# Sinkhorn scaling in a mixing layer: two vectors and two fixed copies of the matrix in place of a matrix scaled in place

## What is computed

```
x_norm = x * rsqrt(mean(x * x) + eps)
H_res_logits = (x_norm @ W_res.T).reshape(B, T, 4, 4) + H_res_base
...
Z = H_res_logits / 0.1
for _ in range(50):                      # Sinkhorn, in logs
    u = -logsumexp(Z + v[..., None, :], axis=-1)
    v = -logsumexp(Z + u[..., :, None], axis=-2)
H_res = exp(Z + u[..., :, None] + v[..., None, :])
H_res = (1 - g) * I + g * H_res          # g = sigmoid(gate)
x_mixed = einsum('btij,btjc->btic', H_res, x_streams)
out = x_mixed + einsum('btc,btn->btnc', (x_pre @ W_branch), H_post)
```

## Time and profile before

| | |
|---|---|
| median of three runs | 2952.16 us (2950.13 to 2953.05) |
| the profiled execution, its own time | 2949.29 us |
| its span, first to last instruction | 2947.6 us |
| mean granted TensorE clock | 0.941 |
| busy share PE, DVE, ACT, POOL | 88%, 62%, 37%, 38% |
| loop of 49 rounds on DVE | 1207.42 to 1384.23 us of the span |
| the mixing of the 16 tiles | 1385.27 to 1491.4 us |

### The profile page before, as it was taken

How to read it: one execution, slowest core, us unless ns; L and a number is a source line. 1 busy time by engine, 2 the same in 40 slices (tenths; PEclk the granted TensorE clock), 3 DMA queues, 4 the chain that set the end, 5 groups by cost and what they waited for, 6 DMA issues and landing times. The chain is left out here.

```text
span 2947.6 us, 50657 instructions
## 1 busy us (share of the span) xinstructions
PE 2588.3 (88%) x15056; PEld 1807.8 (61%) x15056; DVE 1821.9 (62%) x4485; ACT 1082.8 (37%) x2317; POOL 1123.7 (38%) x801
## 2 busy tenths in 40 slices
PE   7999997999998899553759999978999987996999
PEld 6665644765553688542647555536665644885887
DVE  5677775567774433788766766764677773215443
ACT  2345554154555211442511545542355554002000
POOL 7456553555664000000044655536456552002110
PEclk9999998999999899666979999989999998998999
DMA  4323312432320521000134322223232313434111
GB/s 163 102 84 84 95 49 68 147 92 66 102 69 30 180 71 43 0 0 7 80 128 135 86 83 85 79 73 110 77 96 78 103 42 138 141 121 150 65 64 44
DMA packets 121079, 252.95 MB, mean 86 GB/s; under 512 B 12720, under 2 KB 39728, under 8 KB 120880
## 3 DMA queue, kind: packets, MB, share of 16 engines
q1 hardware_dynamic: 120912, 251.03, 26.7%
HBM read 166.57 MB, written 84.41 MB: 85 GB/s over the span
## 5 line engine op out<-in xcount | busy, mean ns | idle before, releaser
L617 ACT ACTIVATE a_prob<-a_pst 128x512 f32<-128x512 f32 (+3 forms) x1536 | 660.9, 493 | 572.2 <-PE a_pst L898 566.4
L710 DVE CUSTOM_DVE_ANT_0 a_psh<-a_psh,a_edge 128x128 f32<-128x128 f32 (+3 forms) x1024 | 480.1, 516 | 198.0 <-PE a_psh L851 170.6
L851 PE MATMUL a_psh<-a_kst,a_qst 127*128 127x512 f32 (+3 forms) x1536 | 485.3, 364 | 26.3 <-DVE a_mx L710 14.4
L898 PE MATMUL a_pst<-a_qst,a_kst 128*128 128x512 f32 (+2 forms) x1536 | 487.2, 372 | 23.1 <-DMA a_qst<-rowmax 18.6
L517 POOL TENSOR_TENSOR a_prob<-a_prob 128x2048 f32<-128x2048 f32 (+1 forms) x96 | 405.6, 4225 | 242.5 <-PE a_ppv L914 242.5
L851 PEld LDWEIGHTS a_psh<-a_kst,a_qst 127*128 127x128 f32 x1536 | 272.4, 189 | 240.2 <-DVE a_mx L713 92.7
L713 DVE TENSOR_REDUCE a_mx<-a_psh 128x1 f32<-128x512 f32 x512 | 329.3, 685 | 127.3 <-PE a_psh L851 126.2
L898 PEld LDWEIGHTS a_pst<-a_qst,a_kst 128*128 128x128 f32 x1536 | 287.5, 194 | 163.9 <-ACT a_prob L617 103.5
L914 PE MATMUL a_ppv<-a_prob,a_vg 128*32 128x512 f32 (+3 forms) x3072 | 319.2, 502 | 0.0
L502 POOL TENSOR_SCALAR_AFFINE_SELECT a_prob<-a_prob 128x512 f32<-128x512 f32 x256 | 161.9, 639 | 188.1 <-ACT a_prob L617 187.9
L927 PE MATMUL a_pden<-a_prob,a_ones 128*32 128x512 f32 (+3 forms) x2304 | 220.1, 475 | 14.1 <-POOL a_prob L517 14.1
(11 more groups left out here) (227 smaller groups left out, 4164.1 us busy)
## 6 DMA issues: line engine op xcount, KB each, us to landing
a_qst<-q SPq DMA_DIRECT2D x192, 256.0 KB, 4.5
a_wraw<-in_wqkv SPq DMA_DIRECT2D x52, 512.0 KB, 4.3
q<-a_stg_hi SPq DMA_DIRECT2D x64, 256.0 KB, 2.1
q<-a_stg_lo SPq DMA_DIRECT2D x64, 256.0 KB, 2.4
a_kst<-kT SPq DMA_DIRECT2D x96, 128.0 KB, 2.6
oT<-a_oT SPq DMA_DIRECT2D x32, 256.0 KB, 2.4
oT<-a_vT SPq DMA_DIRECT2D x32, 256.0 KB, 2.9
h_oraw<-oT SPq DMA_DIRECT2D x16, 512.0 KB, 4.0
```

The costliest lines, as they stand in the source:

```text
L617: act.activation(prob[k % len(prob)][:, h, off:], pst[:, (k * GH + h) % 3, off:], ACT.Exp, scale=scale).then_inc(s["exp_done"], 1)
L710: part = dve.tensor_tensor_reduce(scores, scores, edge[:, BANK - n:], 1.0, 2 * MASKED, ALU.add, ALU.max, mx_hq[kc][:, h, qt:qt + 1])
L851: mm = pe.matmul(psh[:, at, i * n:(i + 1) * n], qst[par][0:P - 1, h, qt * P:(qt + 1) * P], kst[par][0:P - 1, kc * BANK:kc * BANK + n], sta ...
L898: pe.matmul(pst[:, (k * GH + h) % 3, off:], kst[par][:, ki * P:(ki + 1) * P], qst[par][:, h, qc * BANK + off:(qc + 1) * BANK], start=True, ...
```

## The change

The matrix m stays as it is during the 49 rounds. A second tensor mt gets its transpose, once, and two vectors, r64 for rows and v64 for columns, are renewed in turn: the product of one copy and the other vector goes to e, its sums over runs of four go to the vector, and the vector is inverted. `repeated` is a new view of a vector: [128, 16, 4, 4] in which the four numbers of a tile are read as a run, and that run four times. After the rounds g goes into r64, and m is multiplied by both vectors. The two new buffers take 1280 bytes of each partition.

```diff
+        v64 = sb("v64", [P, NT, NS])
+        mt = sb("mt", [P, NT, NS * NS])
...
+        def repeated(v):
+
+            return v.unsqueeze(2).broadcast_to([P, NT, NS, NS])
...
-            def normalise(axis):
-
-                dve.drain()
-                dve.tensor_reduce(r64[:, :, :], lines(m, axis), AX.X, ALU.add)
-                dve.drain()
-                dve.reciprocal(r64[:, :, :], r64[:, :, :])
-                dve.drain()
-                dve.tensor_tensor(lines(m, axis), lines(m, axis), spread(r64[:, :, :]), ALU.mult)
-
-            normalise("col")
+            def scale(kernel, other, out):
+
+                dve.drain()
+                dve.tensor_tensor(lines(e, "row"), lines(kernel, "row"), repeated(other[:, :, :]), ALU.mult)
+                dve.drain()
+                dve.tensor_reduce(out[:, :, :], lines(e, "row"), AX.X, ALU.add)
+                dve.drain()
+                dve.reciprocal(out[:, :, :], out[:, :, :])
+
+            dve.tensor_copy(lines(mt, "row"), lines(m, "col"))
+            dve.tensor_reduce(v64[:, :, :], lines(m, "col"), AX.X, ALU.add)
+            dve.drain()
+            dve.reciprocal(v64[:, :, :], v64[:, :, :])
             with dve.Fori(0, SINKHORN_ITERS - 1):
-                normalise("row")
-                normalise("col")
+                scale(m, v64, r64)
+                scale(mt, r64, v64)
             dve.drain()
 
-            dve.tensor_scalar(m[:, :, :], m[:, :, :], g[:, 2:3], None, ALU.mult)
+            dve.tensor_scalar(r64[:, :, :], r64[:, :, :], g[:, 2:3], None, ALU.mult)
+            dve.tensor_tensor(lines(m, "row"), lines(m, "row"), repeated(v64[:, :, :]), ALU.mult)
+            dve.drain()
+            dve.tensor_tensor(lines(m, "row"), lines(m, "row"), spread(r64[:, :, :]), ALU.mult)
             dve.drain()
```

## The result

The changed kernel takes 2920.99 us (median of five runs, 2918.55 to 2924.47) against 2950.48 us for the kernel before (2948.19 to 2953.05). The ratio is 0.9901 with a 95% interval of 0.9888 to 0.9915.

The account below looks back on a forecast made before the run. DVE's Sinkhorn loop was taken to bound its stretch: rounds -18.0, head -0.2 and tail +0.8 us gave -17.4 us, from 2952.16 to 2934.8 us (87 in 100), with a range of 2930 to 2941 us.

Parts of the forecast that it names:

- What bounds the stretch: From 1342.6 us on, DVE's Sinkhorn loop alone sets the time, so cuts count in full, up to 42 us.
- The rounds: Scaling loop: no half reads in column order any more, saving 0.367 us a round, 18.0 us over 49 rounds.
- Rivals 1 and 2: Loop's product with `repeated` costs 608 ns (about 2953 us, 6 in 100) or 791 ns (about 2971 us, 2 in 100).
- Rival 4: Loop's pauses grow with operation length, so savings count more than once: gain near 36 us, time 2917 us, 1 in 100.
- The head: Before the loop, the copy to mt replaces a product: 1.81 us against 1.99, a gain of 0.2 us.
- The tail: After the loop, g goes into r64, then two products follow: 1.19 us against 0.43, a loss of 0.8 us.
- What is late next: At the turn to mixing: ACT's y leaves 25 us of cover, PE idles some 27 us, clock effect taken as zero.
- The range: Whole kernel: a measured time between 2930 and 2941 us, with less than 2 in 10 left out.
- The price hangs on the read: In the loop's products and reductions, the 183 ns surcharge for column order comes from reading in that order.

## Why the prediction was right in its sum and wrong in its time

- **What bounds the stretch.** Right. All that the loop lost was lost by the stage.
- **The rounds.** Forecast -18.0 us. The time between the first and the last reciprocal fell from 177.4 to 159.3 us, by 18.1. The form that no row of before had, the product with `repeated`, took 425.5 ns where 425 was taken. Rivals 1 and 2 fall on the same row. Rival 4 named 2917 us, near the 2921 measured, but its mechanism didn't occur: the gaps stayed at 74 ns (3.6 us in 49).
- **The head.** Forecast -0.2. The copy took 382 ns and not 602, and the head with the copy in it 1.59 us against 1.99, so -0.4, inside the bound.
- **The tail.** Forecast +0.8. 1.17 us against 0.43, so +0.7.
- **What is late next.** ACT's wait was 25.0 us (25 forecast) and PE's idle time 27.3 (27). DVE's first wait for PE was 4.0 us against 3.7. Over all runs' traces this wait lies anywhere between 2.4 and 4.0 us, with the scaling of the kernel before too (3.9 and 2.5 in two more traces), so neither a gain nor a loss from the clock is shown. The sum of these steps, -17.4, measured -17.9, and the whole kernel with one instruction less came out 17.6 us below the kernel before.
- **The step that failed** is the one that ended the sum with the stage. The prediction asked what each new instruction costs in time and what it waits for, found that "nothing is moved across a queue", and let all later stages stand. But every instruction also has a place, and the change adds one on DVE ahead of a loop of 367 that is run three times for each batch. That loop began on a block's last instruction. There the pauses at the two turns were 6.14 and 5.75 us, where the other places that need loads had 2 to 3. The change moved it to a block's first instruction, where the rounds need no load at all. This was worth 12.5 us in the profiled pair and 11.1 us when a single drain did it, and with the stage's own 17.9 us it makes 29.0 to 30.4 where 29.5 were measured. In the trace of the kernel before it stood as one short row of waits, in a stage without an edit (engine, line, what it waited for: us in total, times, longest):

```profile
DVE a_psh L710 <- issue: 11.9, 2, 6.1
```

- **The range** took in ways in which the stage could go otherwise and none in which another stage could. The last sentence of the prediction, that a later stage whose length moves by over 2 us answers to something outside the sum, is what came true.
- **A side statement was half right.** "The price hangs on the read": the write in 16-byte steps has nearly the same price by itself (187 ns against 178). The change gained by it as forecast, because it took both away.

## What to carry to other kernels

When an edit adds or drops instructions on an engine ahead of a long loop, count how that loop lies before trusting the sum: look in the view of waits for pauses put down to "issue" at the turns of loops, and in the transfers for instruction loads inside rounds. Before a small gain or loss is credited to an edit, run the old kernel with as many idle instructions more or fewer. A layout in which every small operation reads and writes runs can be worth a second copy of the data. Here it saved 183 ns on each product or reduction of 256 numbers, and a product paid about the same (178 to 187 ns) whether the read, the write or both were in 16-byte steps.

## What the runs showed of the hardware

- DVE's instructions come in loads of 8 KB. A loop of 367 instructions needs none in its rounds when it starts 0 or 17 instructions behind an edge, and five in each round at the eight other places seen, 18 to 127; 17 + 367 = 384 is three times 128. That a block is 128 instructions follows from this step, from the positions of the other loops and from the stops at number 128. That one block is loaded ahead of need, so that three are used of four held, explains the five loads for four blocks touched, but was only argued. The Trainium skill (page "Runtime: NRT & Kernel Launch", section "Instruction fetch mechanics") says that most engines, PE not among them, hold two blocks of 16 KiB, 512 instructions, and that a taken branch out of this window forces a load. Four of the 8 KB loads would be its 512, but the runs show only that a loop within three needs none. Its 16 KiB block is not DVE's here; it is what queue 8 shows, 67 packets with 1.10 MB, which by the count of records between them (254 of PE's on average, outside its loops) is PE's.
- The idle time at a turn was 5.75 to 6.15 us when the first block holds one instruction of the loop, 3.1 us at 18, and 2.0 to 2.3 us at the other places seen, with a second stop of 1.2 to 2.1 us at 109 and 110. The first is two pauses one after the other, each with a load beside it; why 18 costs more than 31 is open.
- A loop of 14 instructions over an edge paid 0.12 us in each round, with no load from memory among its rounds.
